# A Mamba block with an FP4 feed-forward layer, written as one software pipeline: the second phase runs one step later, z is each step's last product, and the h transposes fill one row of 768 columns

## The chip, the core and the metric

The kernel runs on one core of one Trainium2 chip. The metric is the device time of one execution in microseconds (us); lower is better. The engines are PE (TensorE: PEld is its weight load), DVE (VectorE), ACT (ScalarE), POOL (GpSimd) and SP (SyncE, which issues the DMAs here). Each runs its own instruction queue in order; semaphores tie them together.

## The reference

x is 8 sequences of 2048 tokens and 256 channels, float32. One state-space layer and one feed-forward layer, each followed by a residual and a layer norm:

```python
xz = x @ W_in; x_proj, z = split(xz, 2)                 # 2 x 512 channels
x_conv = silu(depthwise_conv4(x_proj) + conv_b)
ssm = x_conv @ W_xproj                                   # 33 columns: delta, B (16), C (16)
delta = softplus(ssm[..., 0]); deltaB = delta * B
h_mean = einsum('bld,bln->bdn', x_conv, deltaB) / L      # needs the whole sequence
y = (einsum('bdn,bln->bld', h_mean, C) + D * x_conv) * silu(z)
x = layernorm(x + y @ W_out)
xq = fp4(x); h = silu(xq @ Wg.T) * (xq @ Wu.T)           # 704 columns, FP4 in blocks of 16
x = layernorm(x + fp4(h) @ Wd.T)
```

The mean over the sequence cuts the work in two phases: y of a sequence can start only when all of its x_conv is there.

## The kernel before

**Tiling.** A sequence is four supertiles (`s` = 0..3) of 512 tokens; a supertile has four steps (`j` = 0..3, `TPS`). One step handles one block of 128 channels of the first phase (512 tokens), one block of 128 channels of y, and one tile of 128 tokens of everything behind `W_out`. `walk` (L265) unrolls the four steps of a supertile into `body(i, sg, b, s)` and calls it 38 times; six of the eight sequences run in a loop of the hardware (`fori`, L274). `sg` is the supertile of phase one, `i` = `sg` - 4 that of phase two. In a step `u` = 4 sg + j and `w` = 4 i + j, so the block of y, number `w`, runs 16 steps behind the projection number `u`. Behind it come, in the same step, `v` = u-1 (the silu of the convolution, its product with `W_xproj`), `to` = w-4 (output projection and residual r1), `tx` = w-5 (FP4 of x), `tg` = w-6 (gate and up), `td` = w-7 (transposes of h, down projection) and `tz` = w-8 (output). There are 128 steps of each kind: the first 16 have phase one alone, 112 have both, 16 have phase two alone, and 8 drain.

**PE's order in a step** (`body`, L601): at j = 0 eight transposes of x (L615, into `pa` and `pb`); y (L496); gate and up (L489 into `pgu`, 18 matmuls); the transposes of h, four into bank `pe_` (L631) and two into `pd` (L638), each group with its own signal; the projection of x_proj into `pa`, six matmuls of 512 columns (L489 pa); the same for z into `pb` (L489 pb, `z_product`); for j not 1, the product with `W_xproj` (L571, `state_projection`), which reads `xcs`; the output projection (L537), which overwrites `pd` and so waits until ACT and DVE have copied h's transposes; the transposes of x for the FP4 layer (L548); at j = 1 the partial state (L519) and the transposes of C (L527); the transposes of x_conv (L559); the down projection (L489 pd); at j = 1 `state_projection` stands only here.

**The start of a sequence** (s = 0). y of block 0 needs `h_ready`, which the tail of the previous sequence makes in this very step. `late_y(j, s)` (L301) therefore reorders step j = 0, s = 0: z behind the down projection, then partial state, C, the gate and up of the next step, and y last; step j = 1 then has no gate and up of its own and puts its y behind the h transposes.

**ACT's order in a step** (L727): copy of the four h transposes (L741) and of the two (L744), silu of the gate (L749), `xbig` (L753), silu of the convolution into `xcs` (L760), two copies of the projection (L766, L769), silu of z (L702, `silu_z`), first tap (L777), copy of x's transposes (L782), output norm (L788), copy of x_conv's transposes (L707), h's magnitude (L794), r1's norm (L809). At s = 0, j = 0 silu of z is last but one and waits for the gate on POOL.

**DVE** subtracts the copies (L977, L980), quantises x and h, makes y + D x_conv (`y_skip`, L883), delta B (L890, L894), r1 (L1012) and r2 (L1041). **POOL** multiplies y by silu(z) first in its step (`gate`, L381), then makes the products with the scales (L402 for x, L432 for h) and the rest.

The order of every queue is written by hand; `at_least` and `wait_ge` put the waits. These lines set the wait of L571, and `p2` decides in which steps there is a y:

```python
p1, p2 = exists(sg, NSUP), exists(i, NSUP)
pe.wait_ge(xc_ready, v + 1)          # state_projection, L565
```

## Time and profile before

| | us |
|---|---|
| median of 3 runs (2201.85 to 2204.41) | 2202.8 |
| the profiled execution, its own time | 2204.03 |
| its span on the core | 2202.1 |
| PE busy | 1990.6 (90%) |
| DVE busy | 1756.7 (80%) |
| ACT busy | 1111.5 (50%) |
| POOL busy | 1115.6 (51%) |
| mean granted TensorE clock | 0.98 |

Of the chain of work that ended last, 76% lies on PE and 5% is "issue" (time in which an engine waited for nothing that the profile shows). The timeline view gives start, length and what ended the idle time before it; in it a matmul's length reaches beyond the start of the next, since matmuls are pipelined, and ACT's and DVE's next instruction can start some 0.1 us before the last one's end. The chain view gives each piece its own time without overlap. So a step is best measured from one start to the next of the same kind.

### The profile page before, as it was taken

To read this page: it belongs to the slowest core of one execution; us is meant where nothing else is said; L and a number is where in the kernel's file an instruction comes from. 1 tells how busy PE (TensorE), PEld (TensorE's weight loads), DVE (VectorE), ACT (ScalarE), POOL (GpSimd) and SP (SyncE) were. 2 spreads that over 40 slices of the span, in tenths; PEclk is the share of its full clock that TensorE was granted. 3 is DMA by queue.
4 is the path that set the end of the run, shared out by engine and by line. 5 is a ranking of instruction groups with operands and counts; after the bars stand their busy time and mean duration, and the time that the engine had idled before them with its cause. 6 is when DMAs were issued, how large, how long until landed. Compare 5 with 4: busy or idle time off the path is not lost.

```text
span 2202.1 us, 37847 instructions
## 1 busy us (share of the span) xinstructions
PE 1990.6 (90%) x10532; PEld 1583.8 (72%) x10532; DVE 1756.7 (80%) x3548; ACT 1111.5 (50%) x2100; POOL 1115.6 (51%) x1643
## 2 busy tenths in 40 slices
PE   1887899899999999899999999899999999877776
PEld 1655688688877888688877888688876888666665
DVE  6234788798978888789877888798887888788875
ACT  2665455555545555455544556455544555423332
POOL 2223455466545556455644555465554556445543
PEclk9999999999999999999999999999999999999998
DMA  2111111111111111111111111111111111000000
GB/s 79 50 56 43 34 49 44 44 43 45 49 41 34 44 48 45 36 49 49 41 38 41 44 44 48 38 49 44 39 41 39 49 45 35 29 20 25 20 20 15
DMA packets 77089, 90.53 MB, mean 41 GB/s; under 512 B 8881, under 2 KB 59953, under 8 KB 76849
## 3 DMA queue, kind: packets, MB, share of 16 engines
q1 hardware_dynamic: 76848, 87.73, 12.2%
q8 instruction: 102, 1.67, 0.3%
q14 instruction: 139, 1.13, 0.2%
HBM read 37.37 MB, written 16.78 MB: 25 GB/s over the span
## 4 chain that ended last, share of the span: by engine, by line
PE 76%; issue 5%; DVE 4%; ACT 3%; POOL 1%; ACTq 0%; DVEq 0%; POOLq 0%
PE pgu L489 23%; PE pd L489 14%; PE pd L537 9%; PE pa L489 6%; PE pb L489 6%; PE pc L571 4%; PE pc L519 4%; PE pe_ L631 2%; PE pa L559 2%; PE pc L496 2%; PE pe_ L548 1%; PE pd L638 1%; DVE hbuf L990 1%; DVE qsh L820 1%; PE pa L615 1%
## 5 line engine op out<-in xcount | busy, mean ns | idle before, releaser
L489 PE MATMUL pgu<-wgu_hi,xqT 128*128 128x512 f32 (+1 forms) x1536 | 427.7, 387 | 0.9 <-issue 0.9
L489 PE MATMUL pd<-wd_hi,hqT 128*128 128x256 f32 (+1 forms) x1536 | 334.5, 299 | 18.7 <-DVE r L1012 15.5
L489 PEld LDWEIGHTS pgu<-wgu_hi,xqT 128*128 128x128 f32 x1536 | 279.8, 190 | 75.8 <-issue 27.6
L537 PE MATMUL pd<-wout,g 128*128 128x256 f32 x1024 | 259.9, 398 | 49.6 <-DVE hqT L980 35.2
L489 PEld LDWEIGHTS pd<-wd_hi,hqT 128*128 128x128 f32 (+1 forms) x1536 | 255.8, 190 | 57.4 <-issue 23.8
L946 DVE SCALAR_TENSOR_TENSOR acc<-xps,cw,acc 128x512 f32<-128x512 f32 x256 | 248.7, 972 | 24.4 <-POOL acc L429 23.7
L418 POOL TENSOR_SCALAR rs<-mv 128x1 f32<-128x1 f32 x128 | 61.6, 481 | 396.4 <-DVE mv L1027 228.8
L537 PEld LDWEIGHTS pd<-wout,g 128*128 128x128 f32 x1024 | 191.5, 195 | 79.7 <-issue 56.0
L741 ACT ACTIVATE hqT<-pe_ 128x512 fp32r<-128x512 f32 x128 | 76.2, 595 | 335.3 <-PE pe_ L631 335.3
L402 POOL TENSOR_TENSOR xv<-xnq,qsx 128x256 f32<-128x256 bf16 x128 | 79.5, 621 | 300.1 <-DVE xnq L839 300.1
L489 PE MATMUL pgu<-wgu_lo,xqT 128*128 128x512 f32 (+1 forms) x768 | 228.3, 379 | 0.0
L489 PE MATMUL pd<-wd_lo,hqT 128*128 128x256 f32 (+1 forms) x768 | 217.9, 284 | 0.0
L381 POOL TENSOR_TENSOR g<-g,szr 128x512 f32<-128x512 f32 x128 | 178.5, 1395 | 69.0 <-DVE g L883 69.0
L432 POOL TENSOR_TENSOR hbuf<-hnq,qsh 128x704 f32<-128x704 bf16 x128 | 178.5, 1394 | 13.9 <-DVE hnq L839 13.9
L809 ACT ACTIVATE r<-r,nm,rs 128x256 f32<-128x256 f32 x128 | 76.7, 599 | 204.7 <-POOL nm L422 204.7
L429 POOL TENSOR_TENSOR acc<-acc,tap 128x512 f32<-128x512 f32 x128 | 164.3, 1284 | 16.7 <-ACT tap L777 16.7
L489 PEld LDWEIGHTS pgu<-wgu_lo,xqT 128*128 128x128 f32 x768 | 144.0, 190 | 23.2
L571 PEld LDWEIGHTS pc<-wxp,xcs 128*128 128x128 f32 x1024 | 130.5, 191 | 32.4 <-ACT xcs L760 19.2
L420 POOL TENSOR_TENSOR rs<-rs,nhalf 128x1 f32<-128x1 f32 x128 | 145.1, 1133 | 10.7
L489 PEld LDWEIGHTS pd<-wd_lo,hqT 128*128 128x128 f32 (+1 forms) x768 | 146.6, 191 | 0.0
L571 PE MATMUL pc<-wxp,xcs 128*128 128x33 f32 x1024 | 129.9, 271 | 12.9 <-ACT xcs L760 11.3
L782 ACT ACTIVATE xqT<-pe_ 128x256 fp32r<-128x256 f32 x128 | 49.2, 384 | 176.9 <-PE pe_ L548 176.9
(132 smaller groups left out, 4669.2 us busy)
## 6 DMA issues: line engine op xcount, KB each, us to landing
xcr<-xcs SPq DMA_DIRECT2D x128, 256.0 KB, 2.3
xin<-in_L_attn_x_dram SPq DMA_DIRECT2D x32, 512.0 KB, 3.9
xres<-in_L_attn_x_dram SPq DMA_DIRECT2D x128, 128.0 KB, 2.1
out_dram<-outb SPq DMA_DIRECT2D x128, 128.0 KB, 1.7
szr<-in_L_attn_W_in_dram SPq DMA_DIRECT2D x1, 1024.0 KB, 7.4
szr<-in_L_ffn_w_down_dram SPq DMA_DIRECT2D x1, 704.0 KB, 8.6
szr<-in_L_ffn_w_gate_dram SPq DMA_DIRECT2D x1, 640.0 KB, 4.5
szr<-in_L_ffn_w_up_dram SPq DMA_DIRECT2D x1, 640.0 KB, 5.7
```

The lines of the kernel that those rows point to most:

```text
L381: pool.tensor_tensor(g[:, s % 2, j, :], g[:, s % 2, j, :], szr[:, j, s, :], ALU.mult)\
L402: pool.tensor_tensor(blocks(xv[:, :]), blocks(xnq[:, :]), spread(qsx[:, 1, :]), ALU.mult).then_inc(xprod_done, 1)
L420: pool.tensor_tensor(rs1[:, :], rs1[:, :], nhalf[:, :], ALU.pow).then_inc(rs1_done, 1)
L429: pool.tensor_tensor(acc[:, :], acc[:, :], tap0[:, :], ALU.add).then_inc(tap_done, 1)
L432: pool.tensor_tensor(blocks(hbuf[:, FF:2 * FF]), blocks(hnq[:, :]), spread(qsh[:, 1, :]), ALU.mult).then_inc(hprod_done, 1)
L489: mm = pe.matmul(bank, lhsT, rhs, start=(m == 0), stop=(m == len(pairs) - 1))
L519: mm = pe.matmul(pc[0:H3, :], dB[:, t, :], xct[:, t, :], start=(t == 0), stop=(t == TPS - 1))
L537: mm = pe.matmul(pd[:, 0:DM], g[:, (s + 1) % 2, c, j * P:(j + 1) * P], wout[:, c, :], start=(c == 0), stop=(c == NB - 1))
L571: mm = pe.matmul(pc[:, t * NX:(t + 1) * NX], xcs[:, jb % 2, t * P:(t + 1) * P], wxp[:, jb, :], start=True, stop=True)
L741: act.activation(hqT[:, 0:4, :], pe_[:, :].rearrange("p (c n) -> p c n", c=4), ACT.Copy)\
L809: act.activation(r1[:, j, :], r1[:, j, :], ACT.Identity, bias=nm1[:, :], scale=rs1[:, :])\
L946: dve.scalar_tensor_tensor(acc[:, :], xps[:, k:k + ST], cw[:, jb, k:k + 1], acc[:, :], ALU.mult, ALU.add).then_inc(conv, 1)
```

## The change

- Phase two runs 17 steps behind phase one. The first y of a sequence then falls into step j = 1, whose predecessor has made the state. `late_y` and its reordering go; what remains is that in step s = 0, j = 1 y stands behind the x_proj projection (`mid_y`), and on DVE behind the FP4 of x. Ring positions come from `y_place`. What lies behind y (`to`, `tx`, ...) keeps its distance, so the output projection at j = 0 reads the block that POOL gates in the same step.
- `z_product` is the last product of every step (before the partial state where that is at j = 0). Its silu runs in the next step, on ACT behind the copy of x's transposes, and waits there for that step's gate; the gate stands first on POOL at j = 0 and behind x's scale product at j = 1, 2, 3.
- The six h transposes go into columns 256 to 1023 of one tile `pde` of two banks, with one signal; ACT copies them and DVE subtracts them with one instruction each of 768 columns (two of 512 and 256 before). All six now wait for what the two waited for. The second row of x transposes at j = 0 goes to `pe_` in place of `pb`.

The core of the diff (register arguments and counts that only follow are left out):

```diff
-        pd = ctx.enter_context(nc.psum_tensor("pd", [P, 512], F32))
-        pe_ = ctx.enter_context(nc.psum_tensor("pe_", [P, 512], F32))
+        pde = ctx.enter_context(nc.psum_tensor("pde", [P, 2 * 512], F32))
+        pd = pde[:, 0:512]
+        pe_ = pde[:, 512:1024]
+        hq_cols = pde[:, 1024 - (FC + 1) * P:1024]
...
+        def y_place(i, j, s, b):
+            jy, sy = ring_place(s, j)
+            if j > 0:
+                return i, jy, sy, b
+            return i - 1, jy, sy, (b - 1 if seq_start(s) else b)
...
@@ POOL, body
-                    p1, p2 = exists(sg, NSUP), exists(i, NSUP)
-                    if p2 and not late_y(j, s):
-                        gate(i, j, s, w)
+                    p1, p2 = exists(sg, NSUP), exists(w - 1)
+                    if p2 and j == 0:
+                        gate(i, j, s, b, w - 1)
...
                         pool.tensor_tensor(blocks(xv[:, :]), blocks(xnq[:, :]), spread(qsx[:, 1, :]),
                                            ALU.mult).then_inc(xprod_done, 1)
+                    if p2 and j != 0:
+                        gate(i, j, s, b, w - 1)
...
@@ PE, body
+                    mid_y = j == 1 and seq_start(s)
                     if j == 0 and p1:
                         pe.wait_ge(xin_landed, 16 * (sg + 1))
                         at_least(pe, xct_copied, v)
-                        at_least(pe, z_ready, u)
+                        at_least(pe, xqT_hi, capped(tx, NT))
+                        at_least(pe, xqT_lo, capped(tx, NT))
+                        at_least(pe, hqT_lo, td)
...
-                    after_late = j == 1 and late_y(0, s)
-                    if p2 and not late_y(j, s) and not after_late:
-                        y_product(j, s, b, i, w, capped(v, NT))
-                    if exists(tg) and not after_late:
+                    if p2 and not mid_y:
+                        y_product(i, j, s, b, w - 1, capped(v, NT))
+                    if exists(tg):
                         gate_and_up(tg)
...
-                        for n in range(4):
-                            mm = pe.transpose(pe_[:, n * P:(n + 1) * P],
-                                              hbuf[:, FF + n * P:FF + (n + 1) * P], ident[:, :])
-                        mm.then_inc(hq_pe, 1)
-
+                        if j == 0 and p1:
+                            pe.wait_ge(xt_l, 2 * sg + 2)
                         at_least(pe, r_done, capped(to, NT))
                         at_least(pe, r2_done, td)
-                        for n in range(4, FC + 1):
-                            mm = pe.transpose(pd[:, (n - 4) * P:(n - 3) * P],
-                                              hbuf[:, FF + n * P:FF + (n + 1) * P], ident[:, :])
+                        for n in range(FC + 1):
+                            mm = pe.transpose(hq_cols[:, n * P:(n + 1) * P], hbuf[:, FF + n * P:FF + (n + 1) * P],
+                                              ident[:, :])
                         mm.then_inc(hq_pe, 1)
...
                         projection(pa[:, :], slice(j * P, (j + 1) * P)).then_inc(xp_pe, 1)
-                    if not late_y(j, s) and p1:
-                        z_product(j, s, u, sg)
+                    if p2 and mid_y:
+                        y_product(i, j, s, b, w - 1, capped(v, NT))
                     if j != 1 and exists(v):
                         state_projection(...)
...
                     if j == 1 and exists(v):
                         state_projection(...)
                         transposed_conv(j, jb, sg, u, v, p1)
-                    if late_y(j, s) and p1:
+                    if p1:
                         z_product(j, s, u, sg)
                     if j == 0 and tail_here(j, s, sg):
                         partial_state(sg, w)
                         transposed_c(sg, u + 1 if p1 else u, u)
-                    if late_y(j, s) and exists(tg + 1):
-                        gate_and_up(tg + 1)
-                    if p2 and late_y(j, s):
-                        y_product(j, s, b, i, w, u)
...
@@ ACT, body
-                        act.wait_ge(hq_pe, 2 * td + 1)
-                        act.activation(hqT[:, 0:4, :], pe_[:, :].rearrange("p (c n) -> p c n", c=4), ACT.Copy)\
+                        act.wait_ge(hq_pe, td + 1)
+                        act.activation(hqT[:, 0:FC + 1, :], hq_cols.rearrange("p (c n) -> p c n", c=FC + 1), ACT.Copy)\
                             .then_inc(hqT_hi, 1)
-                        act.wait_ge(hq_pe, 2 * td + 2)
-                        act.activation(hqT[:, 4:6, :], pd[:, 0:2 * P].rearrange("p (c n) -> p c n", c=2),
-                                       ACT.Copy).then_inc(hqT_hi, 1)
...
-                    if not late_y(j, s) and p1:
-                        silu_z(i, j, s, u, w)
...
                         act.activation(xqT[:, 0:KM, :], pe_[:, 0:DM].rearrange("p (c n) -> p c n", c=KM), ACT.Copy)\
                             .then_inc(xqT_hi, 1)
+                    if exists(v):
+                        silu_z(j, s, v, w)
...
@@ DVE, body
-                    if p2 and not late_y(j, s):
-                        y_skip(i, j, s, w)
+                    if p2 and not mid_y:
+                        y_skip(i, j, s, b, w - 1)
...
                     if j == 1 and tail_here(j, s, sg):
                         delta_b(sg)
+                    if p2 and mid_y:
+                        y_skip(i, j, s, b, w - 1)
...
-                    if p2 and late_y(j, s):
-                        y_skip(i, j, s, w)
```

## Rows read from the trace of the kernel before

**Rows 1.** Windows: stretch, length, busy PE PEld DVE ACT POOL, clock, DMA, GB/s.

```profile
1182.40:1242.44 60.04, 59.85 (x329) 48.52 (x329) 53.58 (x110) 33.96 (x65) 37.30 (x55) 1.00 0.14 45
1140.73:1182.40 41.67, 36.86 (x175) 27.41 (x175) 28.49 (x59) 18.75 (x35) 14.06 (x25) 0.92 0.12 40
...
1936.00:2100.00 164.00, 127.54 (x686) 102.71 (x684) 134.23 (x298) 53.17 (x104) 85.00 (x117) 1.00 0.07 22
...
1175.00:1178.00 3.00, 3.00 (x9) 2.15 (x7) 2.35 (x6) 1.58 (x3) 0.62 (x1) 0.50 0.26 93
```

**Rows 2.** Chain of waits, one step (j=3): start, us, what.

```profile
1196.18 0.23 PE pc L496
...
1200.45 0.44 PE pe_ L631 x4
1200.89 0.22 PE pd L638 x2
1201.11 1.39 PE pa L489 x6
1202.50 1.40 PE pb L489 x6
1203.90 0.81 PE pc L571 x8
1204.71 1.81 PE pd L537 x8
...
1207.18 2.52 PE pd L489 x18
```

**Rows 3.** Timeline of ACT there: start, us, instruction, idle before.

```profile
1200.93 0.60 ACT L741 ACTIVATE hqT<-pe_ 128x512 fp32r<-128x512 f32 x1 [3.04 <-PE pe_ L631]
1201.42 0.38 ACT L744 ACTIVATE hqT<-pd 128x256 fp32r<-128x256 f32 x1
1201.68 0.77 ACT L749 ACTIVATE hbuf<-pgu 128x704 f32<-128x704 f32 x1
1202.32 0.43 ACT L753 ACTIVATE xbig<-xv 128x256 f32<-128x256 f32 x1
1202.63 0.64 ACT L760 ACTIVATE xcs<-acc 128x512 f32<-128x512 f32 x1
...
1204.29 0.62 ACT L702 ACTIVATE szr<-pb 128x512 f32<-128x512 f32 x1
```

**Rows 4.** Timeline of DVE in that step.

```profile
1201.86 0.68 DVE L977 TENSOR_TENSOR hqT<-pe_,hqT 128x512 fp32r<-128x512 f32 x1
1202.46 0.41 DVE L980 TENSOR_TENSOR hqT<-pd,hqT 128x256 fp32r<-128x256 f32 x1
```

**Rows 5.** Timeline at s=0, j=0, where z already stands behind.

```profile
1147.03 0.60 PE L631 MATMUL pe_<-ident,hbuf 128*128 128x128 f32 x4
...
1149.37 0.64 ACT L760 ACTIVATE xcs<-acc 128x512 f32<-128x512 f32 x1
...
1150.06 0.97 PE L571 MATMUL pc<-wxp,xcs 128*128 128x33 f32 x7 [0.81 <-ACT xcs L760]
```

**Rows 6.** Timeline of a step j=1.

```profile
1233.23 0.62 POOL L402 TENSOR_TENSOR xv<-xnq,qsx 128x256 f32<-128x256 bf16 x1 [1.17 <-DVE xnq L839]
1233.25 0.81 DVE L894 TENSOR_TENSOR dB<-ssm,delta 128x192 f32<-128x192 f32 x1
...
1234.43 0.63 PE L519 MATMUL pc<-xct,dB 128*48 128x512 f32 x1
```

**Rows 7.** Chain of waits at s=0, j=1.

```profile
1172.01 2.38 issue
1174.39 3.40 PE pd L537 x8
```

**Rows 8.** Timeline of PE where phase two runs alone.

```profile
2004.97 1.97 PE L537 MATMUL pd<-wout,g 128*128 128x256 f32 x8 [1.72 <-DVE hqT L980]
...
2008.46 0.36 PE L489 MATMUL pd<-wd_hi,hqT 128*128 128x256 f32 x1 [0.79 <-DVE r L1012]
```

107 lines of the change are left out of this document (51 added, 56 removed).

## The prediction

> **What bounds the kernel now.** I read the windows first. A supertile inside a sequence takes 60.04 us and PE is busy for 59.85 of them, at full granted clock; DVE, next, is busy for 53.58 [rows 1]. So there PE's own sum is the time: whatever makes PE wait is added, whatever takes a wait from another engine gives nothing. The exception is a sequence's start: from the transposes of x in step j = 0 to y of step j = 2 it takes 41.67 us with PE busy for 36.86 and a mean clock of 0.92 [rows 1]. I then took the chain of waits through one step, which is PE without a gap, and there asked which products lie between a thing that PE produces and the product that needs it back. From the first h transpose PE works 0.44 + 0.22 on the transposes, 1.39 on the x_proj projection, 1.40 on z, and then wants `xcs` for L571; 0.81 later it wants the copied h for L537 [rows 2]. z stands exactly in these gaps.
>
> **z moved to the step's end, j = 0, 2, 3: the term that decides.** ACT starts the h copy when the transposes are done and then runs without a pause: copy, copy, silu of the gate, `xbig`, silu of the convolution. From 1200.93 to the end of the last at 1202.63 + 0.64 = 1203.27 that is 2.34 us [rows 3]. PE has 1.39 of projection behind the transposes and, so far, z's 1.40. Without z, L571 wants to start 0.66 + 1.39 = 2.05 us after the first h transpose [rows 2]. The kernel before shows this very order once in a sequence, where `late_y` has put z behind: first h transpose at 1147.03, `xcs` done at 1150.01, L571 at 1150.06, which is 3.03 us after, with ACT's `xcs` named as the releaser [rows 5]. So the wait is 3.03 - 2.05 = 0.98 us. The order of ACT is not changed ahead of it, and nothing on ACT can start sooner, because it waits for PE's transposes. z still costs its 1.40 at the end of the step, so the wait is a net addition.
>
> **The h transposes in one row.** ACT's copy now starts after six transposes, 0.22 later [rows 2]. The two copies take 0.75 from the start of the first to the start of the silu (1200.93 to 1201.68); 256 columns are worth 0.60 - 0.38 = 0.22, so one copy of 768 is 0.82 long and, with the 0.11 by which ACT's next begins early (0.49 from start to start where the first copy is 0.60 long), 0.71 from start to start [rows 3]. Net 0.22 - 0.04 = +0.18 on the way to `xcs`; the ends are 0 and 0.29 (no overlap). The wait becomes 0.98 + 0.18 = 1.16 us (0.98 to 1.27). DVE's one subtraction, by the same slope, is 0.68 + (0.68 - 0.41) = 0.95 [rows 4]; it ends 0.60 (four transposes, [rows 5]) + 0.22 + 0.82 + 0.95 and a handover or two, about 2.65 us after the first transpose, ahead of L537's new place at 3.21 + 0.81 = 4.02, so it is hidden at j = 0, 2, 3. The earlier waits of the transposes for r1 and r2 of the step before cost nothing: both were met several us earlier, behind gate and up.
>
> Steps with both phases and with h transposes are w = 7 to 111. Of these 79 have j not 1; six are sequence starts that pay already. 73 x 1.16 = **+84.7** (71.5 to 92.7).
>
> **j = 1.** L571 stands at the end there, so `xcs` is hidden. L537 wants to start 2.05 us after the first transpose and gets the subtraction at about 2.7. Behind it the FP4 product of x (POOL, ends 1233.85) and delta B (DVE, ends 1234.06) are needed for L548 and the partial state, which started at 1234.43 [rows 6]. These two are made by a queue that begins with the h subtraction, and that one moves by under 0.2. So PE can be earlier at the partial state by some 0.4 only, and pays z's 1.40 later: +1.0 a step (0.8 to 1.4, the last if nothing comes earlier). 20 such steps outside the sequence starts: **+20** (16 to 28).
>
> **Sequence starts.** Taken away: the 2.38 us in which L537 waits at j = 1, and the half clock behind it (0.50 from 1175 to 1178 [rows 1]), by which the eight matmuls of L537 take 3.40 in place of 1.81 [rows 7, 2]: 3.97 together. What is late next: in step j = 0 the silu of z now runs ahead of softplus on ACT (0.48, the distance from one such start to the next, as L741 to L744 [rows 3]) and the copy chain is 0.18 longer, both on the way to delta B, for which PE waits; in step j = 1 `y_skip` stands between x's FP4 and h's on DVE, so r1 comes later than the down projection wants it, which I put at 0.9. Net 3.97 - 0.48 - 0.18 - 0.9 = 2.4 (0 to 4.0). Eight starts: **-19.2** (-32 to 0). The pause at the loop's turn stays.
>
> **Phase two alone and the drain, 24 steps.** PE waits there for the h copies (1.72) and for r1 (0.79) [rows 8], so the round through ACT sets the time and gets the 0.18: **+4.3** (0 to 7). **Phase one alone, 16 steps:** silu of z leaves ACT's way between the copies and the first tap, at most 0.48 a step, but PE's transposes of x at j = 0 now stand behind z: **-2** (-7.7 to +2).
>
> **POOL, DMA.** The gate at j = 0 is first on POOL, 1.3 us long, and is done some us before that step's output projection; at the other j it follows L402, and silu of z waits for it on ACT, behind which are the output norm, L707 and h's magnitude. ACT has idle time there and PE needs none of these within the step: 0. The save of `xcs` by SP now waits for `yd_done` of the same step, given before the silu is done except at s = 0, j = 1: 0, with one buffer more as cover.
>
> **The sum.** 84.7 + 20 - 19.2 + 4.3 - 2 = +87.8 us. Against the profiled execution, 2204.0 us (span 2202.1; the median of three is 1.2 below), this gives **2292 us**. All low ends together give 2252, all high ends 2334.
>
> **The rivals.**
>
> *A, the waits are covered and only the sequence starts change (0.09): faster.* The place is L571. It decides at 2.05 us from the first h transpose to the end of `xcs`; if the chain through ACT were that short, or if ACT could do the silu of the convolution ahead of the copies, the step would stay 13.5 us, and the 32 us of the starts and 7.7 of phase one would be gained: 2204 - 40 = 2164. For it: z at the end covers the step's boundary, and the starts show 4.8 us in which PE is not busy. Against it: inside a sequence PE has 0.19 us idle in 60 to give back, and rows 5 show 2.98 us where 2.05 would be needed.
>
> *B, the new pauses pull the clock down (0.04).* The half clock behind the wait of 2.38 us made L537's eight matmuls 1.59 longer [rows 7]. Were each of the 79 waits to do so, it would be 79 x 1.59 = +126 on the forecast: 2418. Against it: where phase two runs alone PE pauses for 1.72 and 0.79 us in each step [rows 8], and the granted clock over 164 us of this is 1.00 [rows 1]. The Trainium skill (TensorE: Matmul & The Clock Gate, section "A second HAM failure mode: psum-queue depth-cycling") says that small frequent idle times between groups of matmuls let the clock oscillate between half and full; by that rule this rival would be the outcome, and this trace does not agree, with 1.00 over pauses longer than the new ones.
>
> *C, DVE becomes the round (0.05).* It is busy for 53.58 / 4 = 13.4 us a step [rows 1] and now has to wait for ACT's single copy before it can subtract. The new step of 13.5 + 1.16 leaves 1.3 us for this; every further 0.5 us in each of 104 steps would add 52: 2344. POOL's and DVE's work would have to collide more than now.
>
> *D, the waits are there but about a third of the size (0.04)*, because the starts also return time at the two neighbouring steps: 2225.
>
> **How the numbers follow.** The forecast has 0.78. The range takes in its bounds but for the outermost, and D's side in part: **2240 to 2330**, outside of which lie A, B, C and the tails of the forecast, some 0.2. A measurement of this kernel can tell 0.2% (4.4 us) from no change. Faster 0.10 (A and a corner of D), the same 0.02, slower 0.88.
>
> **What would show it.** The supertile inside a sequence grows from 60.0 to about 64.5 us. Before L571 PE is idle some 1.0 us in every step with j = 0, 2, 3, released by ACT `xcs`; the copy is one of about 0.82 us, the subtraction one of about 0.95. At j = 1 L537 waits for DVE, L519 starts early by less than half a us. The 2.38 us at s = 0, j = 1 go, and the down projection there waits for r1. DVE idles 1 to 1.5 us before the h subtraction. The clock stays at 1.00 inside sequences. If L571 starts with no wait behind the projection, the forecast falls and A holds; if it waits but the supertile doesn't grow, my reading that PE's sum is the time was wrong.

## The result and the profile after

The changed kernel takes **2398.1 us** (median of 4 runs, 2388.9 to 2405.3), the kernel before 2202.3 in the same comparison: a ratio of 1.0885 (95% interval 1.0841 to 1.0929), 8.9% slower. The forecast was 2292 us with a range of 2240 to 2330, so the result lies outside the range. The sign was right, the size less than half of what came: +87.8 us against +189.3 between the two spans (2202.1 and 2391.4).

Lines of the changed kernel, for the rows below: L500 are the split products (in-projections, gate and up, down), L507 y, L648 the h transposes, L582 the state projection, L548 the output projection, L530 the partial state, L559 the transposes of x's FP4, L570 those of the convolution, L629 those of `xin`; on ACT L746 the h copy, L762 `xcs`, L706 the silu of z; on DVE L979 the h subtraction, L823 the FP4 scale, L895 delta B, L1012 the r sums; on POOL L391 the gate.

Windows of the kernel after: a supertile from y to y inside a sequence, a sequence's start (from the transposes of x in j = 0 to y of j = 2), five us of that start, and a stretch of phase two alone. The columns are those of rows 1.

```profile
1280.84:1347.06 66.22, 61.65 (x329) 48.10 (x328) 53.31 (x105) 34.44 (x61) 36.90 (x55) 1.00 0.13 41
1236.22:1280.84 44.62, 38.28 (x174) 26.65 (x174) 30.79 (x58) 19.86 (x35) 16.48 (x27) 0.89 0.11 37
1258.00:1263.00 5.00, 5.00 (x7) 1.22 (x6) 0.45 (x2) 0.00 (x0) 1.06 (x3) 0.50 0.00 0
2165.00:2290.00 125.00, 96.05 (x484) 77.20 (x485) 102.38 (x204) 36.26 (x63) 61.01 (x83) 0.95 0.07 20
```

Against rows 1 the supertile has grown from 60.04 to 66.22 us while PE's instruction count (329) is the same: PE, idle for 0.19 us before, now waits for 4.6, and is busy for 1.8 us longer with the same instructions. In the five us of the start the clock is at its lower level (0.50, 1.2 of 2.4 GHz). The start has gone from 41.67 to 44.62. What PE waits for, in the waits of the kernel after (engine and line, releaser, us in total, times, longest):

```profile
PE pc L582 <- ACT xcs L762: 101.7, 90, 2.4
PE pde L548 <- DVE hqT L979: 54.9, 45, 2.1
PE pde L500 <- DVE r L1012: 36.8, 67, 1.7
...
PE pc L530 <- DVE dB L895: 20.7, 11, 3.1
```

The first line is the wait that the forecast named (L571 in the old numbering): 90 times, 1.13 us each. The third, 36.8 us in 67 waits, was 15.5 in 22 in the kernel before; the forecast had it longer at one step of a sequence's start alone. The first and the third stand in one step, here j = 3 from the timeline of the kernel after (start, length, idle before it and its releaser):

```profile
1300.78 0.82 PE L648 MATMUL pde<-ident,hbuf 128*128 128x128 f32 x6
1301.35 0.70 PE L500 MATMUL pa<-xt_hi,win_hi 128*128 128x512 f32 x2
...
1304.15 1.05 PE L582 MATMUL pc<-wxp,xcs 128*128 128x33 f32 x8 [1.17 <-ACT xcs L762]
1305.03 1.97 PE L548 MATMUL pde<-wout,g 128*128 128x256 f32 x8
...
1307.85 0.36 PE L500 MATMUL pde<-wd_hi,hqT 128*128 128x256 f32 x1 [0.19 <-DVE r L1012]
```

```profile
1301.63 0.81 ACT L746 ACTIVATE hqT<-pde 128x768 fp32r<-128x768 f32 x1 [5.71 <-PE pde L648]
1302.34 0.75 ACT L751 ACTIVATE hbuf<-pgu 128x704 f32<-128x704 f32 x1
...
1303.28 0.63 ACT L762 ACTIVATE xcs<-acc 128x512 f32<-128x512 f32 x1
...
1302.48 0.96 DVE L979 TENSOR_TENSOR hqT<-pde,hqT 128x768 fp32r<-128x768 f32 x1 [1.80 <-ACT hqT L746]
1305.89 1.07 DVE L823 TENSOR_SCALAR qsh<-qsh 128x44 f32<-128x44 f32 x1
...
1305.65 1.27 POOL L391 TENSOR_TENSOR g<-g,szr 128x512 f32<-128x512 f32 x1
```

ACT runs copy, silu, `xbig`, `xcs` without a pause to 1303.91; L582 follows 0.24 later. The copy (0.81) and the subtraction (0.96) have the forecast lengths (0.82, 0.95). The last two lines are the surprise: a DVE instruction on 44 elements a partition takes 1.07 us, and ends at 1306.96, just as POOL's gate ends (1306.92).

### The profile page after: what moved, and what is told of

It is laid out like the page before. It is cut to its first block, busy times and chain, and to the rows that moved or that the text cites. A ratio compares the mean times of both kernels' runs of the same rounds, so it can differ in the third digit from the quotient of the medians.

```text
span 2391.4 us, 37362 instructions
## 1 busy us (share of the span) xinstructions
PE 2077.4 (87%) x10532; PEld 1600.9 (67%) x10532; DVE 1764.7 (74%) x3420; ACT 1121.6 (47%) x1972; POOL 1111.5 (46%) x1643
## 3 DMA queue, kind: packets, MB, share of 16 engines
q8 instruction: 98, 1.61, 0.3%
## 4 chain that ended last, share of the span: by engine, by line
PE 50%; DVE 14%; issue 10%; ACT 7%; POOL 3%; ACTq 0%; DVEq 0%; POOLq 0%
PE pgu L500 17%; PE pde L500 10%; PE pb L500 5%; PE pde L548 4%; PE pc L530 4%; PE pc L582 3%; PE pde L648 3%; DVE hqT L979 2%; DVE qsh L823 2%; ACT hqT L746 2%; DVE qsh L820 2%; DVE hbuf L988 2%; PE pc L507 1%; POOL hbuf L445 1%; ACT xcs L762 1%
## 5 line engine op out<-in xcount | busy, mean ns | idle before, releaser
L500 PE MATMUL pgu<-wgu_hi,xqT 128*128 128x512 f32 (+1 forms) x1536 | 425.4, 385 | 0.0
L500 PE MATMUL pde<-wd_hi,hqT 128*128 128x256 f32 (+1 forms) x1536 | 339.9, 303 | 40.9 <-DVE r L1012 36.8
L746 ACT ACTIVATE hqT<-pde 128x768 fp32r<-128x768 f32 x128 | 104.1, 813 | 537.2 <-PE pde L648 537.2
L548 PE MATMUL pde<-wout,g 128*128 128x256 f32 x1024 | 284.4, 426 | 54.9 <-DVE hqT L979 54.9
L500 PEld LDWEIGHTS pgu<-wgu_hi,xqT 128*128 128x128 f32 x1536 | 278.0, 188 | 76.1 <-issue 28.8
L500 PEld LDWEIGHTS pde<-wd_hi,hqT 128*128 128x128 f32 (+1 forms) x1536 | 259.9, 193 | 80.3 <-issue 47.4
L979 DVE TENSOR_TENSOR hqT<-pde,hqT 128x768 fp32r<-128x768 f32 x128 | 122.5, 957 | 199.3 <-ACT hqT L746 199.3
L548 PEld LDWEIGHTS pde<-wout,g 128*128 128x128 f32 x1024 | 202.8, 208 | 95.9 <-issue 68.8
L582 PE MATMUL pc<-wxp,xcs 128*128 128x33 f32 x1024 | 138.8, 281 | 103.0 <-ACT xcs L762 101.7
L500 PE MATMUL pgu<-wgu_lo,xqT 128*128 128x512 f32 (+1 forms) x768 | 227.2, 377 | 0.0
L582 PEld LDWEIGHTS pc<-wxp,xcs 128*128 128x128 f32 x1024 | 127.4, 195 | 146.5 <-issue 77.9
L500 PE MATMUL pde<-wd_lo,hqT 128*128 128x256 f32 (+1 forms) x768 | 220.2, 287 | 0.0
L391 POOL TENSOR_TENSOR g<-g,szr 128x512 f32<-128x512 f32 x128 | 172.6, 1349 | 18.2 <-DVE g L884 18.0
L500 PEld LDWEIGHTS pgu<-wgu_lo,xqT 128*128 128x128 f32 x768 | 143.0, 188 | 22.9
L836 DVE SCALAR_TENSOR_TENSOR hbuf<-hbuf 128x704 f32<-128x704 f32 x128 | 114.3, 893 | 59.0 <-ACT hbuf L796 53.9
L500 PEld LDWEIGHTS pde<-wd_lo,hqT 128*128 128x128 f32 (+1 forms) x768 | 149.0, 194 | 0.0
L530 PE MATMUL pc<-xct,dB 128*48 128x512 f32 x256 | 131.0, 660 | 20.7 <-DVE dB L895 20.7
```

Source lines behind the costliest of these rows:

```text
L391: pool.tensor_tensor(g[:, sy % 2, jy, :], g[:, sy % 2, jy, :], szr[:, jy, sy, :], ALU.mult)\
L500: mm = pe.matmul(bank, lhsT, rhs, start=(m == 0), stop=(m == len(pairs) - 1))
L530: mm = pe.matmul(pc[0:H3, :], dB[:, t, :], xct[:, t, :], start=(t == 0), stop=(t == TPS - 1))
L548: mm = pe.matmul(pde[:, 0:DM], g[:, (s + 1) % 2, c, j * P:(j + 1) * P], wout[:, c, :], start=(c == 0), stop=(c == NB - 1))
L582: mm = pe.matmul(pc[:, t * NX:(t + 1) * NX], xcs[:, jb % 2, t * P:(t + 1) * P], wxp[:, jb, :], start=True, stop=True)
L746: act.activation(hqT[:, 0:FC + 1, :], hq_cols.rearrange("p (c n) -> p c n", c=FC + 1), ACT.Copy)\
```

## The experiments

Totals are medians; the supertile is the window from y to y inside a sequence, where one was read.

| kernel | us | ratio to before (95%) | supertile |
|---|---|---|---|
| before | 2202 to 2204 | 1 | 60.04 |
| the change | 2398.1 | 1.0885 (1.0841 to 1.0929) | 66.22 |
| z_last_alone | 2358.8 | 1.071 (1.0692 to 1.0728) | 65.43 |
| gate_later_alone | 2257.4 | 1.0253 (1.0233 to 1.0272) | 60.42 |
| two_h_copies | 2367.7 | 1.0731 (1.0671 to 1.0791) | 65.55 |
| xcs_first | 2354.7 | 1.0672 (1.0633 to 1.0712) | 65.58 |
| gate_first | 2384.9 | 1.0833 (1.0805 to 1.086) | 65.81 |
| xcs_first_gate_first | 2301.6 | 1.044 (1.0422 to 1.0458) | 64.43 |
| z_before_down | 2270.2 | 1.0315 (1.0296 to 1.0335) | 62.67 |
| z_first_again | 2392.1 | 1.085 (1.0826 to 1.0874) | - |
| z_first_two_copies | 2378.2 | 1.0801 (1.0777 to 1.0825) | - |
| z_three_times_at_start | 2399.5 | 1.0907 (1.0876 to 1.0937) | - |
| before_silu_z_later | 2199.6 | 0.9985 (0.9972 to 0.9998) | - |
| before_two_moves | 2199.5 | 0.9985 (0.9975 to 0.9995) | - |

**One part alone: z last.** The kernel before, with z's projection behind the down projection and its silu in the next step.

```diff
-                    if not late_y(j, s) and p1:
-                        z_product(j, s, u, sg)
...
                     if exists(td):
                         down_projection(to, td)
...
+                    if p1:
+                        z_product(j, s, u, sg)
```

> The kernel before, with z alone moved: z is the last product of every step (ahead of the partial state at s = 0, j = 0), its silu runs in the next step behind the copy of x's transposes, and the second row of x transposes goes to pe_. Phase two stays 16 steps behind, the h transposes stay in two rows, the gate stays first on POOL. Theory 1 (L571 waits for the silu of the convolution because z no longer covers it): a wait of about 1.0 us in front of L571 at j = 0, 2, 3, 0.3 to 0.4 us of exposed weight loads around the new place of z, +0.9 at j = 1; supertile inside a sequence about 65 us, in all about 2320 us. The steps with phase two alone stay at 12.70 us, since the gate has not moved. Rival (the loss of the changed kernel comes from the gate's new place on POOL and from the later phase two, z costs little): about 2210 to 2240 us, supertile under 61.5.

(The second row of `xin` goes to `pe_` there, since `pb` still holds z.) Measured: 2358.8, +155 us, some four fifths of the whole and 39 above the expectation. Windows, and one step of PE's timeline:

```profile
1337.49:1402.92 65.43, 61.60 (x329) 48.11 (x328) 52.74 (x109) 34.57 (x65) 35.19 (x52) 1.00 0.12 41
```

```profile
1357.05 0.60 PE L635 MATMUL pe_<-ident,hbuf 128*128 128x128 f32 x4
...
1360.27 0.49 PE L571 MATMUL pc<-wxp,xcs 128*128 128x33 f32 x3 [1.00 <-ACT xcs L763]
```

From the first h transpose to L571 it takes 3.22 us, where the forecast had 3.03. In the forecast's sense (less 2.05) the wait is 1.17, where it had 0.98; the 1.00 in the row is the idle time that the profile shows, and belongs beside the 0.81 of rows 5. So the mechanism stands, the wait is 0.19 longer, and the supertile grows by 5.4 us, not by 3 x 0.98 + 1.0 = 3.9. Laid beside a step j = 2 of the kernel before (starts of neighbouring groups in the timeline), the projection ahead of L571 and the wait are +1.17, L571 itself +0.07, the down projection +0.08 (its next is now z, not y), z 1.59 in place of 1.40, and the steps' two other edges +0.03: +1.54 in all. A quarter of it is small joints, not the wait. And the seven starts between the supertiles inside sequences grow by 31 us in all here, with `late_y` and the lag of 16 still in place: PE waits 3.53 us before L537 at s = 0, j = 1 (2.38 before) and 2.69 for delta B (1.08 before). The step of phase two alone stays at 12.70.

**One part alone: the gate's place.** The kernel before, with POOL's gate behind the history copy and the product of x.

```diff
-                    if p2 and not late_y(j, s):
-                        gate(i, j, s, w)
                     if p1:
...
                                            ALU.mult).then_inc(xprod_done, 1)
+                    if p2 and not late_y(j, s):
+                        gate(i, j, s, w)
```

> The kernel before with one GpSimd instruction moved: the gate product stands behind the history copy and the x product, as in the changed kernel, and not first (late gates at the first step of a sequence as before). Theory: there it runs beside the FP4 scale operation L823 of VectorE, which takes 1.07 us in place of 0.17, so that the r1 sum and the down projection are late; the steps of phase two alone, which have no in-projection to cover it, go from 12.70 to 13.4 to 13.75, the total rises by 15 to 60 us, to 2218 to 2265. Inside the sequences the gain or loss is below 0.3 us a step. Rival: the stretching of L823 belongs to the changed kernel's timing, not to the gate's place; then the total stays at 2200 to 2212.

Measured: 2257.4, +54 us, inside the expectation. Phase two alone, in its trace: PE, DVE and POOL of one step.

```profile
2038.07 0.36 PE L489 MATMUL pd<-wd_hi,hqT 128*128 128x256 f32 x1 [1.66 <-DVE r L1012]
...
2036.12 1.06 DVE L823 TENSOR_SCALAR qsh<-qsh 128x44 f32<-128x44 f32 x1
2037.56 0.36 DVE L1012 TENSOR_TENSOR r<-pd,xres 128x256 f32<-128x256 f32 x1
...
2035.88 1.26 POOL L381 TENSOR_TENSOR g<-g,szr 128x512 f32<-128x512 f32 x1
```

In the kernel before the same three stand like this:

```profile
2020.08 0.19 DVE L823 TENSOR_SCALAR qsh<-qsh 128x44 f32<-128x44 f32 x1
2020.65 0.36 DVE L1012 TENSOR_TENSOR r<-pd,xres 128x256 f32<-128x256 f32 x1
...
2015.36 1.27 POOL L381 TENSOR_TENSOR g<-g,szr 128x512 f32<-128x512 f32 x1
```

The scale operation ends when the gate ends (2037.18 and 2037.14), so r1 comes 0.87 later and the down projection waits 1.66 in place of 0.79 [rows 8]; a step of phase two alone takes 13.58 in place of 12.70. Inside the sequences it costs 0.4 us a supertile, and at most of the starts the steps around the product of y are some 5 us longer, much of it at a clock of 0.83 to 0.86. The mean clock of this kernel is 0.968, that of the kernel before 0.980: over spans of 2255 and 2202 us this is 72 and 44 us of missing clock, so up to half of the +53 could be the clock that the longer pauses cost. The 0.88 of phase two alone is not: there the clock is 1.00 in this kernel too (2033 to 2083).

The Trainium skill (SBUF — State Buffer, section "SBUF: two separate sides") describes a pair of ports shared by VectorE and GpSimd, an exclusive lock that an instruction holds to its end, against VectorE instructions with two SBUF inputs or in a two-port mode. The ends above agree with such a lock, and so does every other case in the trace of the changed kernel: of the 128 L823 on 44 elements, 92 lie beside the gate, and each of them ends within 0.05 us of its end, 65 of them 1.06 to 1.08 us long; the other 36 take under 0.2, as all 128 do in the kernel before, where none lies beside it. L823 has one input, and no row shows in which mode it ran.

**One part undone: the row of 768.** The changed kernel with four h transposes in `pe_`, two in `pd`, two copies and two subtractions.

```diff
-                        mm.then_inc(hq_pe, 1)
+                            if n in (3, FC):
+                                mm.then_inc(hq_pe, 1)
...
-                        act.wait_ge(hq_pe, td + 1)
-                        act.activation(hqT[:, 0:FC + 1, :], hq_cols.rearrange("p (c n) -> p c n", c=FC + 1), ACT.Copy)\
+                        act.wait_ge(hq_pe, 2 * td + 1)
+                        act.activation(hqT[:, 0:4, :], pe_[:, :].rearrange("p (c n) -> p c n", c=4), ACT.Copy)\
```

> The changed kernel with the h transposes back in two rows (four blocks in pe_, two in pd), so with two signals, two ACT copies and two VectorE subtractions as in the kernel before; everything else of the change stays. My theory prices the one row of 768 columns at +0.18 us in every step whose critical chain runs transposes, copy, subtraction, down projection, because all six transposes must end before the one copy begins. It expects the steps of phase two alone at 12.70 where the gate stands first (12.86 in the changed kernel), about 0.1 to 0.2 us less per step, and a total of 2365 to 2385 (the changed kernel: 2398). Rival: one copy and one subtraction save as much in fixed cost as they lose in overlap, then the total stays at 2390 to 2400.

Measured: 2367.7, -30 us against the changed kernel. The steps of phase two alone fall from 12.86 to 12.70 and from 13.75 to 13.58, j = 2 and 3 by 0.16 and 0.17. That is the 0.18 of the forecast, in the place it was put. 128 steps at 0.17 would be 22; the rest is of the size of the scatter of these two kernels (2349 to 2372 and 2389 to 2405).

**Two repairs, alone and together.** `xcs_first` puts the silu of the convolution ahead of ACT's h copy; `gate_first` puts the gate back to the front of POOL's step (not at s = 0, j = 1).

```diff
+                    if exists(v):
...
+                        act.activation(xcs[:, jb % 2, :], acc[:, :], ACT.Silu).then_inc(xc_ready, 1)
                     if exists(td):
                         act.wait_ge(hq_pe, td + 1)
```

```diff
-                    if p2 and j == 0:
+                    if p2 and not (j == 1 and seq_start(s)):
                         gate(i, j, s, b, w - 1)
```

> The changed kernel, with one instruction of ACT moved: the silu of the convolution (xcs) stands ahead of the h copy, where ACT sits idle for 5 us. The wait in front of L582 must go in every step with j = 2, 3. If that wait was the only thing that made the step long, it falls from 15.55 to about 14.3 us and the total to about 2290. Rival, which I hold likelier from the changed kernel's trace: r1 (DVE L1012) is made 6.9 us after the first h transpose whatever PE does, because the gate on POOL holds DVE's L823 for 1.07 us, and the down projection needs it at 7.0; then the pause only moves from L582 to the down projection, the step stays at 15.4 to 15.55 and the total at 2380 to 2400.

> The changed kernel, with POOL's gate first in every step but s = 0, j = 1 (as in the kernel before), silu of z unchanged behind it. Theory (the gate at its new place collides with DVE's L823, 1.07 in place of 0.17 us, and r1 is late by that): the steps with phase two alone fall from 13.75 to 12.86 us, as those with j = 0 are already; the wait of the down projection at j = 2, 3 (0.19 us) goes; L582's wait of 1.17 us stays. Total 2350 to 2365. If the late r1 has nothing to do with the gate: 2393, steps of 13.75.

> Both edits together. If two chains stand side by side (ACT to L582 and DVE to the down projection), either alone gives little and both give the whole: step j = 2, 3 about 14.6 us in place of 15.55, supertile about 62.5 to 63.5 in place of 66.2, total 2270 to 2300. If they are independent, the gains of the two single runs add up.

Measured against the changed kernel: -43, -13 and together -97 us. The first lies between the two totals expected (2290, or 2380 to 2400), the second (2384.9) above its 2350 to 2365, the third (2301.6) just above its 2270 to 2300. The waits of PE in `xcs_first`:

```profile
PE pde L500 <- DVE r L1012: 101.3, 103, 1.7
PE pde L548 <- DVE hqT L979: 59.4, 50, 2.1
```

in `gate_first`:

```profile
PE pc L582 <- ACT xcs L762: 103.6, 92, 2.8
...
PE pde L500 <- DVE r L1012: 18.7, 25, 1.6
```

and with both:

```profile
PE pde L548 <- DVE hqT L979: 63.4, 58, 2.1
PE pde L500 <- DVE r L1012: 44.8, 104, 1.7
```

`xcs_first` takes 88 of the 102 us of L582 away, and the down projection then waits 101 us for r1: step j = 2 stays at 15.55. `gate_first` halves r1's wait and leaves L582's: the step goes to 15.40. Only both together make it clearly shorter, 14.66. Two chains ran side by side in the same step, one over ACT and one over DVE and POOL, and the longer one hid the other. Step j = 0, with the gate first in every kernel of these, gains from `xcs_first` alone (15.20 to 14.60); and 22 of the 43 us of `xcs_first` lie at the starts, where the wait for delta B falls from 2.7 to 1.29 in four of seven. `gate_first` misses its expectation in part by the clock: where phase two runs alone its step is 12.86 as expected in five of fourteen cases, and 13.5 to 13.8 in the other nine, at a clock of 0.87 or 0.88.

**z ahead of the down projection.** Both repairs, and z in between the transposes of the convolution and the down projection, its silu right behind the first tap.

```diff
+                    if p1 and not mid_y:
+                        z_product(j, s, u, sg)
                     if exists(td):
                         down_projection(to, td)
```

> The kernel with both the xcs silu ahead of the h copy and the gate first on GpSimd (2301.6, step j = 2 at 14.65), and now z's projection back ahead of the down projection and its silu right behind the first tap, so that of the change only the lag of 17, the one h row and the table of signals are left. My theory prices z behind the down projection at 0.7 to 0.9 us per step that has z: with z ahead, TensorE has 1.4 us of work between the state projection and the down projection, which covers the wait for the h copy and subtraction. It expects the step j = 2 at 13.8 to 14.0 and the supertile at 61 to 62, total 2215 to 2260. Rival: what is left of the slowing (14.65 against 13.65 in the kernel before) is the row of 768 columns and the falls of the clock; then step j = 2 stays above 14.4 and the total at 2285 to 2305.

Measured: 2270.2, ten us above the expectation; j = 2 is 13.78, as expected, the supertile 62.67 (61 to 62 was expected). So z's place in front of the down projection is worth another 31 us. A part of what is left shows in its waits:

```profile
PE pde L548 <- DVE hqT L983: 79.7, 74, 2.1
```

The output projection waits for the h subtraction, in a supertile 1.3 us at j = 1, 0.4 at j = 3 and nothing at j = 2; the kernel before has 35.2 us in 19 such waits, nearly all where phase two runs alone. Here z covers r1, not the h copies: for those it would have to stand ahead of L548. I had not thought of that when I wrote the expectation.

**z in its old place, with the lag of 17.** Both repairs, z ahead of the state projection, its silu behind `xcs` in the next step; the second kernel has two h copies besides.

```diff
+                    if z_early:
+                        z_product(j, s, u, sg)
                     if j != 1 and exists(v):
                         state_projection(j, jb, sg, v, w)
```

> The kernel with both the xcs silu ahead of the h copy and the gate first on GpSimd (2301.6), and now z's projection back in its old place on TensorE, right behind the first in-projection and ahead of the state projection; its silu still stands a step later (the lag of 17 needs that), now right behind the xcs silu, ahead of the h copy. The one h row of 768 columns stays. (At the first two steps of a sequence z keeps a later place.) My theory says that z's 1.4 us of TensorE work ahead of the state projection are the cover of xcs and of the h copy and subtraction, and that the lag itself costs nothing: the step j = 2 falls from 14.65 to 13.55 to 13.85, the supertile to 60 to 61, the total to 2205 to 2250. Rival: the lag of 17, with the silu a step later, has a price of its own (ACT waits for the gate of the step before the h copy); then step j = 2 stays above 14.2 and the total above 2260.

> The kernel z_first_again with the h transposes back in two rows (two signals, two ACT copies, two VectorE subtractions). What is left of the change then is the lag of 17 with y of the step before, z's silu a step later, and z's place at the first two steps of a sequence. Theory: 0.16 to 0.18 us per step where the chain through the h transposes is critical, so the steps of phase two alone go from 12.86 to 12.70 and the total falls by 5 to 17 us against z_first_again, to 2195 to 2235. Rival: inside the sequences z's product covers that chain, only the 32 steps at the end gain, and the two totals are within 5 us of each other.

Measured: 2392.1 and 2378.2, both far from my expectation. The difference of the two, 14 us, is within the 5 to 17 expected. Of the rival the price and its cause hold, but not its place: step j = 2 is 13.7, as the theory had it, and PE waits for the silu of z at j = 0, 1 and 3 (0.8, 1.8 and 1.5 to 1.8 us). Timeline of the first, j = 0:

```profile
1396.73 0.71 PE L500 MATMUL pa<-xt_hi,win_hi 128*128 128x512 f32 x2
...
1399.16 0.50 PE L500 MATMUL pb<-xt_hi,win_hi 128*128 128x512 f32 x1 [0.79 <-ACT szr L711]
...
1398.51 0.60 ACT L711 ACTIVATE szr<-pb 128x512 f32<-128x512 f32 x1 [0.39 <-POOL g L391]
...
1396.63 1.84 POOL L391 TENSOR_TENSOR g<-g,szr 128x512 f32<-128x512 f32 x1
```

```profile
PE pb L500 <- ACT szr L711: 120.1, 83, 5.2
```

With phase two 17 steps behind and room for 16 results of z, the silu of z may only write when the gate of the step has read its place, so it runs a step late, and until then `pb` holds z. z can't be projected again before; that is 120 us of waiting. So the lag is no free part of the change: with this one bank and this ring it asks for z near the end. A longer ring or a second bank for z was not run.

**The clock at a sequence's start.** The changed kernel with z's product done three times at j = 0 of a sequence's start, in the time in which PE waits for delta B.

```diff
-                projection(pb[:, :], slice(DI + j * P, DI + (j + 1) * P)).then_inc(z_pe, 1)
+                for _ in range(times):
+                    mm = projection(pb[:, :], slice(DI + j * P, DI + (j + 1) * P))
+                mm.then_inc(z_pe, 1)
```

> The changed kernel with z's projection done three times over at the first step of each sequence, j = 0 (the same product into the same bank; 2.8 us more of TensorE work, eight times, inside the stretch in which TensorE waits 2.7 us for dB anyway). My theory: the partial state behind that wait runs 6.56 us instead of 3.57 because the granted clock has fallen to half when it begins, after a stretch of waits. If TensorE has work in place of the idle time, the clock stays at 1.00 there, the partial state takes about 3.6 us and the total falls by 8 x 2 to 3 us, to 2370 to 2385. Rival: the fall comes from waits further ahead (those of 1.6 us for xcs) and is there whatever is done in the gap; then the extra product itself runs at half clock, 2.8 to 5.6 us of work stand where 2.7 us of wait were, and the total stays or rises to 2398 to 2425.

The changed kernel, PE at one such start, the one with the longest partial state:

```profile
1246.35 3.61 PE L548 MATMUL pde<-wout,g 128*128 128x256 f32 x8
...
1257.52 6.63 PE L530 MATMUL pc<-xct,dB 128*48 128x512 f32 x8 [2.74 <-DVE dB L895]
```

and with the product three times:

```profile
1248.48 1.97 PE L550 MATMUL pde<-wout,g 128*128 128x256 f32 x8
...
1258.01 3.63 PE L532 MATMUL pc<-xct,dB 128*48 128x512 f32 x8
```

In this kernel PE comes to the partial state from work in the six starts before the last, and it takes 3.63 us in each; in the changed kernel it takes 5.0 to 5.3 in five of them and 6.63 in this one, 10.9 us more in all. 2.8 us of additional work cost nothing there. The pause alone does not decide it: `z_last_alone` has a wait of 2.69 at the same place and 3.63 behind it in four of seven starts. Yet the total is the same, 2399.5, which is the rival's number (2398 to 2425) but not by the rival's way. The gain is lost at the loop's turn, ahead of the transposes of `xin`: PE's waits have "PE pa L629 <- issue: 4.7, 5, 1.5" in the changed kernel, and here

```profile
PE pa L631 <- issue: 18.7, 5, 4.6
```

Behind this longer pause the clock is at half for the gate and up products. The kernel before has 14.3 us in 5 such waits, so the change itself had gained 9.6 us at the loop's turn, and this kernel gives it back. The change's longer starts are in part the clock's, but the run doesn't put a price on the whole. In 2.80 us of this pause (1233.10 to 1235.90) PE and ACT are idle, and the only DMA queues that move anything are those for instructions:

```profile
q8 instruction: 1, 0.02, 2.3%
q14 instruction: 2, 0.02, 2.0%
```

The Trainium skill (Runtime: NRT & Kernel Launch, section "Instruction fetch mechanics") says that a taken branch out of the prefetched code has to fetch its target by DMA first. That fits these lines; why the pause is 0.9 us on the mean in one kernel and 3.7 in the next stays open.

**The kernel before, its starts.** First the late silu of z moved from the end of step j = 0 behind the h copies of j = 1; then, besides, `xcs` ahead of the h copies at s = 0, j = 0.

```diff
+                    if j == 1 and late_y(0, s) and p1:
+                        silu_z(i, 0, s, u - 1, w - 1)
...
-                    if late_y(j, s) and p1:
-                        silu_z(i, j, s, u, w)
```

> The kernel before with one ACT instruction moved: at the first step of each sequence the late silu of z (which waits for the product of z and y there) goes from the end of step j = 0 to step j = 1, behind the h copies. In the kernel before ACT stands at that instruction while the r1 norm and the h copies are queued behind it, and TensorE waits 2.38 us for them at s = 0, j = 1 and falls to half clock. My theory of the sequence starts (queue order on ACT, not the amount of work) expects that wait gone and 3 to 5 us less per sequence start: 2165 to 2185. Rival: the wait only moves to the next product that needs an ACT result, and the total stays at 2200 to 2210.

> The kernel before_silu_z_later (2199.6) with one more ACT instruction moved: at the first step of each sequence alone, the xcs silu stands ahead of the h copies. There TensorE waits 0.81 us for it in the kernel before (1.70 in before_silu_z_later) and runs the state projection and the output projection behind it at half clock. Theory: that wait goes, seven or eight times, and with it some of the half clock: 6 to 20 us less, 2180 to 2194, which beats the kernel before by 0.4 to 1%. Rival: the pause only moves to the next product that waits, the output projection, and the total stays within 4 us of 2199.6.

Measured: 2199.6 and 2199.5, 0.15% faster (0.9972 to 0.9998, 0.9975 to 0.9995) and so the same within 2%; expected were 2165 to 2185 and 2180 to 2194. The rivals hold: L537 at s = 0, j = 1 still waits 2.16 us, in place of 2.38, in both, and in the second the 0.81 before L571 are gone in four of six starts without a gain. In the first, DVE comes earlier to its work at j = 1 and then meets the gate:

```profile
1166.71 0.41 DVE L820 TENSOR_REDUCE qsx<-r 128x16 f32<-128x256 f32 x1
1167.04 1.68 DVE L946 SCALAR_TENSOR_TENSOR acc<-xps,cw,acc 128x512 f32<-128x512 f32 x1
...
1170.64 0.41 DVE L980 TENSOR_TENSOR hqT<-pd,hqT 128x256 fp32r<-128x256 f32 x1
...
1166.87 1.29 POOL L381 TENSOR_TENSOR g<-g,szr 128x512 f32<-128x512 f32 x1 [0.22 <-DVE g L883]
```

In the kernel before DVE waits 1.07 us for the r1 norm ahead of L820, and L946 takes 0.74:

```profile
1170.87 0.42 DVE L820 TENSOR_REDUCE qsx<-r 128x16 f32<-128x256 f32 x1 [1.07 <-ACT r L809]
1171.21 0.74 DVE L946 SCALAR_TENSOR_TENSOR acc<-xps,cw,acc 128x512 f32<-128x512 f32 x1
...
1173.88 0.41 DVE L980 TENSOR_TENSOR hqT<-pd,hqT 128x256 fp32r<-128x256 f32 x1
```

So the wait of 1.07 turns into 0.94 of L946 being held beside the gate. And the "issue" of rows 7 has an owner: the h subtraction L980 ends at 1174.29 and L537 starts at 1174.39. The 2.38 us were DVE's queue, not ACT's copies, which had been done since 1171.53.

## Why the prediction was right in sign and wrong in size

The span of the profiled execution, cut at the same events in both kernels:

| part | forecast | measured |
|---|---|---|
| 21 supertiles inside sequences | 21 x 4.48 = +94 | +130 |
| the seven starts between them | -9 | +33 |
| phase two alone and the drain | +4 | +17 |
| up to the first output projection | -2 | +9 |
| sum | +87.8 | +189.3 |

(The forecast's 93 steps are 84 in the 21 supertiles and 9 beside the starts, some 10 us, which the second line holds with the -19.2. Of the +130, 118 are in 18 supertiles, 6.6 each (6.2 where the clock stays at 1.00), and 11 in the three of the first sequence, in which the pipeline still fills.)

*Right:* the bound (PE's sum; a wait added to it is added to the time), the mechanism and its place (90 waits before the state projection, ACT `xcs` the releaser), the 0.18 of the row of 768 (0.16 to 0.17), the length of copy and subtraction, j = 1 (+0.91 for +1.0), the end of the 2.38 us and r1 late at s = 0, j = 1 (1.64 us, for 0.9). Rival A falls: with `xcs` ahead of the copies, its second condition, the step stayed at 15.55 and the total was 2354.7.

Three steps of it failed: the wait of 1.16 us was too small, the gate's move on POOL was put at nothing, and the starts had the wrong sign.

*The step of 1.16, mis-sized.* 84.7 us of the forecast hang on this term. It measures 1.55, 1.90 and 1.80 at j = 0, 2, 3. Of the 1.90 at j = 2, 1.32 is the wait in the forecast's sense (1.17 with z alone, for 0.98): I took the 0.05 of rows 5, a step j = 0, for the handover from `xcs` to L571. In the trace of after it is 0.05 in 41 waits, those at j = 0 (1.61 and 0.98 long), and 0.24 in 46, those at j = 2 and 3, for which the trace of before held no case. Why these differ, no run tells. Another 0.3 are joints (L582 and the down projection 0.07 and 0.06 longer, z 1.59 for 1.40). I moved z "at its 1.40", the pitch it had between two products of the same kind. The last 0.23 is r1.

*POOL, at zero: wrong.* The step in the text was that "at the other j it follows L402" and that PE needs nothing behind it within the step. I asked who waits for the gate, and not beside what it runs. There, L823 stands, and behind it r1 and the down projection. On its own that is +54 us (`gate_later_alone`), up to half of it by the clock; taken back out of the change it is 13, and 53 once `xcs` is first. It costs 0.2 in the step and 0.88 in phase two alone: 12.86 at j = 0, where the gate is first, is 12.70 + 0.16 and close to the forecast, and 13.75 is that and the held L823.

*The starts, -19.2: wrong in sign.* The 2.38 went, as said. But PE's wait for delta B, 1.08 in the kernel before, is 2.2 to 2.9 in the six starts before the last, where the forecast had added 0.66, and the partial state behind it, 3.63 in the kernel before, takes 5.0 to 5.3 and once 6.63, for which the forecast had no term. Before L582 PE waits 0.98 to 2.1 at j = 0, in place of 0.8 in most, and the output projection of that step takes 1.97 in three of the seven starts and 2.6 to 3.6 in the other four (1.97 in six of seven before). The longer wait for delta B comes with z's move: `z_last_alone`, without the lag, the row or the gate's move, has 2.69 for it. It also has +31 in the same seven stretches, with no more clock missing there than before (19 us for 24), but 1.15 of each is L537's longer wait, which the change does not have; so how the rest of the +33 divides, no run tells. `xcs_first` alone gives 22 us back over the seven, probably because `xcs` no longer stands on ACT behind `xbig`, which waits for DVE and its delayed scale. "The pause at the loop's turn stays" was wrong too, the other way: 14.3 us in 5 turns went to 4.7, and the +33 are what is left after this gain.

*"The clock stays at 1.00 inside sequences":* true of the supertile above, 1.00 with a pause of 1.17 in two of its steps and of 0.98 in a third, but not of all. In 5 of the 72 steps of the 18 full supertiles the changed kernel shows 0.90, the kernel before in none, and each is 1.2 to 1.5 us longer. Two steps j = 3, and two of phase two alone:

```profile
1362.70:1379.13 16.43, 15.07 (x87) 12.46 (x86) 13.48 (x28) 7.63 (x14) 9.33 (x13) 1.00 0.10 34
1428.91:1446.78 17.87, 16.72 (x86) 13.56 (x85) 13.51 (x28) 7.53 (x14) 9.33 (x13) 0.90 0.09 31
2226.06:2239.81 13.75, 9.90 (x56) 7.96 (x54) 11.25 (x22) 4.03 (x7) 6.64 (x10) 1.00 0.06 20
2198.47:2212.32 13.85, 11.37 (x56) 9.19 (x54) 11.35 (x22) 4.03 (x7) 6.63 (x10) 0.88 0.05 14
```

Nor is it true of the starts (0.89) and of phase two alone (0.95 for 1.00). Span times mean clock misses 44 us before (0.980 of 2202) and 93 after (0.961 of 2391), so rival B holds in part, with at most 49 of the 189 us. Some 20 of the 49 lie in phase two alone and the drain, where they cost next to nothing: with 0.88 the step takes 13.85 for 13.75, since PE waits for r1 there anyway. In `z_last_alone` the mean is 0.978, 52 us missing, and the time is +149: the bulk is not the clock.

*Phase one alone, -2 for +9:* `xin`'s transposes stand behind z and its silu there. The direction was named, the size not. It is z's place: the first output projection starts at 227.7 us in the changed kernel, at 230.3 in `z_last_alone`, and at 218.4 both in the kernel before and in `gate_later_alone`.

The range failed because its outer ends varied each term within its own rows, and held no end for an operation that is slowed by a neighbour, or for a clock that falls more often: all high ends together gave 2334.

## What to carry to other kernels

Where the busiest engine runs without a gap, a product of it that seems free to move is the cover of whatever other engines do beside it: count, for each place that it leaves, what the next product there waits for. When an instruction moves on GpSimd, read which VectorE instructions it will run beside, not only who waits for it. And undo two suspects together as well as each alone: here -43 and -13 were -97 together, because each had hidden the other.

## What the runs showed of the hardware

- A VectorE instruction of 0.17 to 0.19 us takes 1.06 to 1.07 beside a GpSimd product of 1.27, and ends within 0.05 us of it (92 of 92 in the changed kernel); one of 0.74 with two SBUF inputs takes 1.68.
- A TensorE product that has stood waiting for the same ACT result starts 0.05 us after its end in one step of the loop and 0.24 in two others (41 and 46 waits of the changed kernel).
- With a pause of some 1.2 us in steps of 15 to 16 us the granted clock is 1.00 in most steps and 0.90 in 5 of 72, which are 1.2 to 1.5 us longer. In phase two alone it is 0.95 in the changed kernel, where each step has a pause of 2.09 and three in four a second of 1.66; it is 1.00 with 1.72 and 0.79 in the kernel before [rows 1, 8] and with 1.73 and 1.66 in `gate_later_alone`. Of the rule that small idle times between groups of matmuls let the clock oscillate (the Trainium skill, TensorE: Matmul & The Clock Gate, section "A second HAM failure mode: psum-queue depth-cycling") most supertiles show nothing; the five steps and phase two alone after the change agree with it.
- A step with the clock at 0.87 or 0.88 in phase two alone is 0.1 us longer in the changed kernel (13.85 for 13.75), where PE waits 1.66 for r1 behind the output projection in the steps at full clock, and 0.6 longer in `gate_first` (13.5 for 12.86), where that wait is 0.78.
- At the loop's turn PE stands for 1.6 to 3.4 us in the kernel before, for 0.6 to 1.5 in the changed kernel, and for 3.3 to 4.6 in that one with 12 more matmuls in the loop's code.
